# Attention rows cut into two halves, the second half of one row issued beside the first half of the next

## The chip, the cores and the metric

One core of a Trainium2 chip runs the whole program. The metric is the device time of one execution in microseconds (us); lower is better. The engines are TensorE (PE in the profile), VectorE (DVE), ScalarE (ACT), GpSimd (POOL) and SyncE (SP), which here issues most of the DMAs.

## The reference

The input x is float32 of shape 32 x 64 x 112 x 112. Four residual layers follow each other, each on a group-normalised copy of its input:

```
x = x + local_conv(gn(x))          # sign(x) with ternary 3x3 weights
x = x + fourier_mix(gn(x))         # rfft2, complex 64x64 channel mix, irfft2
x = x + conv7x7(gn(x)) + bias      # written as FFTs in the reference
x = x + window_attention(gn(x))    # 8x8 windows, 8 heads of 8 channels
```

The last layer, per window of 64 tokens, is linear attention:

```
q, k, v = split(xw @ qkv_w.T + qkv_b);  k = k + pos_enc
q, k    = relu(q) + eps, relu(k) + eps, both / softplus(scale)
q, k    = cubed, rescaled to their old norms
kv      = k.T @ v (per head);  out = (q @ kv) / (q . mean(k) + eps)
out     = out + depthwise5x5(v);  out = out @ proj_w.T + proj_b
```

## The kernel before

The program has three stages. The first two (local convolution with the forward transform, and the channel mix) end at about 3,230 us of the trace and are not touched. The third, `large_conv_and_attention`, runs over the 32 images and does the inverse transform, the 7x7 convolution and the attention.

An image in this stage has two parts. `bring(n)` makes layer 2's result for image n: 16 groups of first transform products (line 937) that ScalarE copies out (L1077), 14 groups of second products (L950) that VectorE adds to x (L1248), the statistics, and the first four padded chunks of the convolution's input. `both(n)` then runs seven rows. A row does one seventh of image n's convolution on TensorE (204 matmuls of 128x224 in float16, L913) and, between them, one row of 14 windows of attention of image n-1. Matmuls of the convolution are the filler: a table of numbers (`PIECES`, `FIRST_PIECES`, `SECOND_PIECES`) says how many of the 204 have been issued before each attention step.

There is no scheduler. Each engine has its own program, written in order by hand and executed in that order; they meet at counting semaphores. What stands first on an engine holds up everything behind it.

The attention steps of a row l, in the order of TensorE before the change:

- `project` (L976): q, k, v of the 14 windows in four groups into PSUM banks 2 to 5. VectorE's `take_qkv` adds the biases (L1318, L1322) and then does the relu (L1330).
- depthwise product (L992) into banks 4 and 5.
- ScalarE squares q and k (L1152). GpSimd makes the cubes of q (L1480), VectorE those of k (L1346). TensorE transposes the query cubes (L1000); ScalarE copies them to `qt` (L1166).
- ScalarE squares the cubes (L1160), VectorE sums them (L1350), makes the ratio of the norms and scales the keys (L1358).
- key-value products (L1011), masked by VectorE into `kvm` (L1368); numerator (L1023).
- VectorE: reciprocal of the denominator (L1374, L1379), multiply (L1384), add the depthwise result (L1391).
- TensorE transposes the result back (L1031), ScalarE copies it (L1171), TensorE projects it (L1041), ScalarE writes `o2` (L1178, which the profile shows as the tile c_kvm since they share memory), GpSimd adds it to x (L1485), SyncE stores it.

The convolution has its own traffic in a row. It makes nine products p = 0 to 8 in four rotating PSUM banks. ScalarE takes the first three into `bs` (`take_b`, L1141 and L1144). VectorE takes the other six (`take_t`, L1299 and L1302); p = 7 and 8 of a row are taken at the start of the next one. GpSimd's `add_conv` (L1464, L1468) adds them to x, and its second half needs all six takes of that row; when it is done it counts up `x3_done`. `take_b` of the next row waits for that count, since it overwrites `bs`. For the next image's convolution ScalarE pads (L1107), GpSimd and VectorE take differences (L1450 to L1455, L1276, L1277), ScalarE rounds to float16 (`high_part`, L1118), and VectorE keeps the remainder (`low_part`, L1284); the two slots of `tn` are used in turn, so padding chunk k waits for `low_part` of chunk k-2.

## Time and profile before

| | |
|---|---|
| median of 3 runs | 13081.69 us (13077.68 to 13088.68) |
| the profiled execution's own time | 13098.74 us, span of its trace 13097.1 us |
| busy share of the span | PE 81%, PE weight loads 71%, DVE 62%, ACT 45%, POOL 27% |
| convolution matmuls, L913 | 45,696 of them, 5004.8 us busy |
| mean granted TensorE clock | 0.908 |

In a trace row, the first number is the start in us from the span's start, the second the time until the group's last instruction ends, then the engine, the line of the kernel, the operation, out <- in, the shapes and xN, the number of instructions merged. A float32 matmul is recorded as two. In square brackets stands the idle time of that engine just before, and what ended it. Instructions of one engine overlap at their ends by about 0.1 us.

A row of the view of stretches gives the stretch, its length, then the busy time of PE, PE's weight loads, DVE, ACT and POOL, each with its number of instructions, and last the granted TensorE clock (1.00 is 2.4 GHz, 0.50 is 1.2 GHz), the DMA share and GB/s.

### The profile page before, as it was taken

The page shows a single profiled execution, that of the slowest core. Times are in us where ns is not written, and L with a number is a line of the kernel's source. Part 1 is how long each engine was busy: PE and PEld are TensorE (multiplying, and loading weights), DVE is VectorE, ACT ScalarE, POOL GpSimd, SP SyncE. Part 2 cuts the span into 40 slices and gives each one's busy share as a digit, 9 for nine tenths or more (in the row PEclk, how much of TensorE's full clock was granted, in tenths as well). Part 3 has the DMA queues.
Part 4 walks back from the last instruction along what each step waited for, and adds up shares of the span by engine and source line. Part 5 has one row for each costly group of instructions (what it writes and reads, how often), then busy time and mean ns, then how long its engine had stood idle before and what let it go on. Part 6 is the DMA issues. An engine that isn't in the chain of part 4 may idle for free.

```text
span 13097.1 us, 288527 instructions
## 1 busy us (share of the span) xinstructions
PE 10575.0 (81%) x120871; PEld 9276.6 (71%) x120871; DVE 8077.5 (62%) x14156; ACT 5870.0 (45%) x6792; POOL 3544.7 (27%) x2888
## 2 busy tenths in 40 slices
PE   6888878857888888888888888888888888888885
PEld 4666668856777777777777777777777777777774
DVE  6666622144666666666666666666666666666665
ACT  4555521103444445444444444445454444444442
POOL 0000000002333333333333333333333333333331
PEclk9999988878999999999999999999999999999996
DMA  7888889952111111111111111111111111111100
GB/s 187 214 213 220 209 189 240 245 142 54 34 32 33 33 32 34 32 34 32 34 32 33 34 33 44 40 35 32 33 34 32 32 34 32 34 32 34 32 21 15
DMA packets 969161, 946.98 MB, mean 72 GB/s; under 512 B 588704, under 2 KB 933776, under 8 KB 948176
## 3 DMA queue, kind: packets, MB, share of 16 engines
q1 hardware_dynamic: 944400, 708.58, 24.6%
q0 software_dynamic: 23488, 220.21, 4.7%
q8 instruction: 947, 15.52, 0.5%
q14 instruction: 326, 2.67, 0.1%
HBM read 605.77 MB, written 322.96 MB: 71 GB/s over the span
## 4 chain that ended last, share of the span: by engine, by line
PE 31%; DVE 17%; ACT 13%; issue 10%; POOL 4%; DMA 1%; ACTq 0%; DVEq 0%; POOLq 0%; SPq 0%
PE c_ps L913 18%; ACT c_tn L1107 3%; PE c_ps L976 3%; ACT c_xn L1128 2%; PE c_ps L1011 2%; ACT c_kvm L1178 2%; POOL c_cube L1480 2%; PE c_ps L1023 2%; DVE c_s L1350 2%; PE c_ps L1031 2%; DVE c_qk L1330 2%; PE c_ps L1041 2%; DVE c_xp L1284 2%; DVE c_xr L1248 2%; DVE c_inv L1379 1%
## 5 line engine op out<-in xcount | busy, mean ns | idle before, releaser
L913 PE MATMUL c_ps<-c_xp,c_wst 128*128 128x224 f16 x45696 | 5004.8, 268 | 474.4 <-DVE c_xp L1284 474.4
L913 PEld LDWEIGHTS c_ps<-c_xp,c_wst 128*128 128x128 f16 x45696 | 4443.5, 100 | 940.0 <-issue 626.9
L1464 POOL TENSOR_TENSOR c_xr<-c_sm,c_xr 128x448 f32<-128x448 f32 x448 | 616.8, 1377 | 4040.9 <-DVE c_xr L1302 4040.9
L1107 ACT ACTIVATE c_tn<-c_xr,c_nrm 64x448 f32<-64x448 f32 (+1 forms) x960 | 1098.9, 1145 | 145.5 <-DVE c_xp L1284 128.6
L1171 ACT ACTIVATE c_qt<-c_ps 128x896 f32<-128x896 f32 x224 | 205.5, 917 | 2018.1 <-PE c_ps L1031 2018.1
L1450 POOL TENSOR_TENSOR c_tn<-c_tn 128x224 f32<-128x224 f32 (+1 forms) x480 | 594.5, 1239 | 1656.8 <-ACT c_tn L1107 1656.8
L528 PE MATMUL b_ps<-b_xs,b_wt 64*64 64x64 f32 x6384 | 802.5, 299 | 181.1 <-DVE b_xj L504 172.3
L1302 DVE SCALAR_TENSOR_TENSOR c_xr<-c_ps,c_unscale,c_xr 128x224 f32<-128x224 f32 x896 | 546.9, 629 | 611.4 <-PE c_ps L913 611.4
L528 PEld LDWEIGHTS b_ps<-b_xs,b_wt 64*64 64x64 f32 x6384 | 757.5, 219 | 185.5 <-issue 185.3
L1118 ACT ACTIVATE c_xp<-c_tn 128x1080 f16<-128x1080 f32 (+1 forms) x544 | 572.3, 1063 | 662.4 <-DVE c_tn L1277 656.1
L976 PE MATMUL c_ps<-c_wqkv,c_xn 64*128 64x192 f32 x6272 | 757.9, 374 | 118.5 <-ACT c_kvm L1178 62.6
L528 PE MATMUL b_ps<-b_xj,b_wt 64*64 64x64 f32 x6384 | 806.5, 298 | 12.2 <-issue 12.0
L528 PEld LDWEIGHTS b_ps<-b_xj,b_wt 64*64 64x64 f32 x6384 | 767.0, 222 | 13.8 <-issue 13.7
L976 PEld LDWEIGHTS c_ps<-c_wqkv,c_xn 64*128 64x128 f32 x6272 | 547.4, 204 | 289.7 <-issue 92.2
L1178 ACT ACTIVATE c_kvm<-c_ps,c_pbias 64x448 f32<-64x448 f32 x896 | 563.4, 629 | 362.3 <-PE c_ps L1041 353.8
L1480 POOL TENSOR_TENSOR c_cube<-c_sq,c_qk 128x896 f32<-128x896 f32 x224 | 657.7, 2936 | 230.7 <-ACT c_sq L1152 230.7
L1299 DVE SCALAR_TENSOR_TENSOR c_sm<-c_ps,c_unscale,c_bs 128x224 f32<-128x224 f32 x448 | 201.8, 451 | 821.3 <-PE c_ps L913 752.6
L1284 DVE TENSOR_TENSOR c_xp<-c_tn,c_xp 128x1080 f16<-128x1080 f32 (+1 forms) x544 | 695.5, 1290 | 14.2 <-ACT c_xp L1118 14.2
L1318 DVE TENSOR_TENSOR c_qk<-c_ps,c_bqk 128x512 f32<-128x512 f32 (+1 forms) x896 | 557.0, 622 | 236.2 <-PE c_ps L976 228.1
L1152 ACT ACTIVATE c_sq<-c_qk 128x1792 f32<-128x1792 f32 x224 | 380.3, 1698 | 702.9 <-DVE c_qk L1330 702.1
L1350 DVE TENSOR_REDUCE c_s<-c_sq 128x28 f32<-128x1792 f32 x224 | 452.5, 2020 | 384.4 <-ACT c_sq L1160 384.4
L1128 ACT ACTIVATE c_xn<-c_xr,c_nrm 64x448 f32<-64x448 f32 x896 | 675.7, 754 | 24.8 <-DVE c_nrm L1233 15.9
(155 smaller groups left out, 18064.6 us busy)
## 6 DMA issues: line engine op xcount, KB each, us to landing
b_wt<-in_L_conv_weight SPq DMA_DIRECT2D x56, 2048.0 KB, 21.8
a_xc<-in_x SPq DMA_DIRECT2D x64, 1568.0 KB, 18.7
x<-a_x1s POOLq DMA_DIRECT2D x32, 3136.0 KB, 23.1
a_xh<-x SPq DMA_DIRECT2D x64, 1568.0 KB
c_xr<-x SPq DMA_DIRECT2D x32, 3136.0 KB, 11.2
out<-c_xr SPq DMA_DIRECT2D x448, 224.0 KB, 3.1
xf<-a_freq POOLq DMA_DIRECT2D x32, 1792.0 KB, 17.5
b_xs<-xf SPq DMA_DIRECT2D x28, 2048.0 KB, 25.2
```

The costliest lines, as they stand in the source:

```text
L528: ins = pe.matmul(ps[rows, 4 * half + g % 4, at:at + 2 * B], wt[rows, odd, :, f, r], src[rows, odd, :, f], start=(f == lo and r == 0), sto ...
L913: ins = pe.matmul(sums(c, p), wst[:, ws, pr, FIRST_TAP[p] + k].rearrange("p q o -> p (q o)"), xp[:, xs, PLANE[kind] + f, row:row + CROWS, ...
L976: ins = pe.matmul(ps[:, banks[g] + r, 3 * C * (q % 2):3 * C * (q % 2) + 3 * C], xn[rows, 2 * q:2 * q + 2].rearrange("p w t -> p (w t)"), w ...
L1107: ins = act.activation(put[to, :, a - lo:b - lo], get[of, :, a - first:b - first], ACT.Identity, scale=nrm[of, 0, 0:1], bias=nrm[of, 0, 1:2])
L1118: ins = act.activation(xp[:, 0, :, at:at + rows].rearrange("p k j w -> p k (j w)"), tn[:, k % 2, 0:9, 0:rows].rearrange("p k j w -> p k (j ...
L1128: ins = act.activation(xn[C * wr:C * wr + C].rearrange("p w (j hp x) -> p hp j w x", hp=2, x=WS)[:, hp], xr[C * hp:C * hp + C, odd, 8 * a ...
L1178: ins = act.activation(o2[C * hp:C * hp + C].rearrange("p (r b j) x -> p b r j x", r=2, b=2)[:, y], ps[C * y:C * y + C, 4:6, 0:N4].rearran ...
L1284: ins = dve.tensor_tensor(xp[:, 1, :, at:at + rows].rearrange("p k j w -> p k (j w)"), tn[:, k % 2, 0:9, 0:rows].rearrange("p k j w -> p k ...
L1350: dve.tensor_reduce(sums(s6), squares(sq), AX.X, ALU.add).then_inc(s.s6_done, 1)
L1450: pool.tensor_tensor(tn[:, k % 2, E_AT:E_AT + 3:2, 0:hi - lo, 1:1 + QW], tn[:, k % 2, X0_AT:SLOTS:X2_AT - X0_AT, 0:hi - lo, 1:1 + QW], at( ...
L1464: pool.tensor_tensor(here, apart(sm[:, half]).unsqueeze(1).to_broadcast([P, 2, CROWS, QW]), here, ALU.add).then_inc(s.added, 1)
L1480: pool.tensor_tensor(cube[:, :, 0].rearrange("p q r c -> p r q c"), sq[:, :, :, 0], qk[:, :, :, 0], ALU.mult).then_inc(s.q3_done, 1)
```

## The change

The second half of a row, from the numerator to the output, is moved. It is now issued during the first half of the next row (or, for the seventh row of an image, during `bring`). The functions are split for that: `numerator`, `turn_back`, `give_back` on TensorE, `turned` and `give` on ScalarE, `divide`, `multiply`, `add_depthwise` on VectorE, `add_out` on GpSimd.

- Banks: the projection now uses banks 2 and 3 for all four groups, each after VectorE has taken the one before. Depthwise product, key-value products, numerator and the turned result use banks 4 and 5. The first and second transform products use the convolution's four banks.
- The depthwise result is copied out of PSUM by ScalarE (a new 128x896 instruction per row, L1227 of the new kernel), and added by VectorE in one instruction from SBUF where there were two from PSUM.
- `take_b` moves ahead on ScalarE, in front of `turned` and of the square. On VectorE the takes of p = 6, 7, 8 of the row before stand behind the relu; p = 7 and 8 stood in front of `take_qkv`, p = 6 in the row before.
- In `bring`, VectorE's four takes of q, k, v are mixed with the differences and low parts.
- x is loaded in seven pieces, each after the rows of output that it overwrites have been stored, where one load waited for the whole image.
- The table of pieces has new numbers.

That VectorE makes the key cubes is so in both kernels.

The table and TensorE's program:

```
-PIECES = (12, 30, 62, 114, 130, 168, 184)
+PIECES = (14, 26, 38, 52, 72, 112, 188)
...
             def bring(n, odd):
+                row = (n - 1) * A7
+                if above_zero(row):
+                    numerator(row - 1)
...
                 for g in range(16):
+                    if above_zero(row):
+                        if g == 4:
+                            turn_back(row - 1)
+                        if g == 8:
+                            give_back(row - 1)
...
+            def attend(l, a, conv):
+                pieces = PIECES if a else FIRST_PIECES
+                if a:
+                    project(l, 0)
+                    numerator(l - 1)
+                    for g in range(1, 4):
+                        conv(pieces[g - 1])
+                        project(l, g)
+                    conv(pieces[3])
+                    turn_back(l - 1)
+                    conv(pieces[4])
+                    give_back(l - 1)
+                conv(pieces[5])
```

On ScalarE:

```
             def attend(l, a, odd, conv, pad, high):
+                pad()
+                conv(True)
+                if a:
+                    turned(l - 1)
+                act.wait_ge(s.u_done, l + 1)
+                if above_zero(l):
+                    act.wait_ge(s.s6_done, l)
+                    act.wait_ge(s.att_done, l)
+                act.activation(sq[:], qk[:], ACT.Square).then_inc(s.u2_done, 1)
+                if a:
+                    give(l - 1)
+                high(0)
+                conv(False)
```

On VectorE:

```
             def attend(l, a, conv, conv_before, pad, stats):
+                if a:
+                    take_qkv(l, 0)
+                    divide(l - 1)
+                    take_qkv(l, 1)
+                    multiply(l - 1)
+                    take_qkv(l, 2)
+                    add_depthwise(l - 1)
+                    take_qkv(l, 3)
+                    relu(l)
+                conv_before(6)
                 conv_before(7)
                 conv_before(8)
-                if a:
-                    take_qkv(l, a)
```

On SyncE:

```
+            def load_next(t, odd, a):
+                p = (odd + a) % 2
+                sp.wait_ge(out_done[p], (A7 * t + ((A7 * odd + a - p) // 2 + 1)) * 32)
+                sp.nop(nofuse=True)
+                load_x1(2 * t + (2 + odd), odd, a)
```

What stands on TensorE around the two last steps of a row. Before (L1031 turns back, L1041 projects, L976 projects q, k, v of the next row):

```order
L913 MATMUL c_ps<-c_xp,c_wst 128x224 x25
L1031 MATMUL c_ps<-c_ident,c_qt 128x128 [waits c_att_done]
L1031 MATMUL c_ps<-c_ident,c_qt 128x128 x6
L913 MATMUL c_ps<-c_xp,c_wst 128x224 x16
L1041 MATMUL c_ps<-c_qt,c_wproj 64x448 [waits c_back_taken]
L1041 MATMUL c_ps<-c_qt,c_wproj 64x448 x3
```

After (L1010 turns back, L1020 projects; L989 is the fourth projection group of the next row, L1041 its query transposes):

```order
L989 MATMUL c_ps<-c_wqkv,c_xn 128x192 [waits c_qk_taken]
L989 MATMUL c_ps<-c_wqkv,c_xn 128x192
L922 MATMUL c_ps<-c_xp,c_wst 128x224 x10
...
L1010 MATMUL c_ps<-c_ident,c_qt 128x128 [waits c_att_done]
...
L922 MATMUL c_ps<-c_xp,c_wst 128x224 x20
L1020 MATMUL c_ps<-c_qt,c_wproj 64x448 [waits c_back_taken]
...
L922 MATMUL c_ps<-c_xp,c_wst 128x224 x24
...
L1041 MATMUL c_ps<-c_ident,c_cube 128x128 [waits c_q3_done]
```

Both steps have moved from the end of their own row to behind the fourth projection group of the next one; 20 convolution matmuls stand between them where there were 16.

On ScalarE, from the padding at a row's start (L1107 before, L1140 after). Before:

```order
L1107 ACTIVATE c_tn<-c_xr,c_nrm 64x4x4x28 [waits c_lo_done]
...
L1152 ACTIVATE c_sq<-c_qk 128x1792 [waits c_s6_done,c_u_done]
L1128 ACTIVATE c_xn<-c_xr,c_nrm 64x4x14x8 [waits c_qkv_done]
...
L1118 ACTIVATE c_xp<-c_tn 128x9x120 [waits c_prod_done]
...
L1141 ACTIVATE c_bs<-c_ps,c_unscale 128x448 [waits c_x3_done,c_prod_done]
L1160 ACTIVATE c_sq<-c_cube 128x1792 [waits c_s2_done,c_k3_done,c_q3_done]
```

After (L1174 is `take_b`, L1182 `turned`, L1206 the square, L1191 `give`, L1214 the square of the cubes):

```order
L1140 ACTIVATE c_tn<-c_xr,c_nrm 64x4x4x28 [waits c_lo_done]
...
L1174 ACTIVATE c_bs<-c_ps,c_unscale 128x448 [waits c_x3_done,c_prod_done]
L1182 ACTIVATE c_qt<-c_ps 128x896 [waits c_turned_back]
L1206 ACTIVATE c_sq<-c_qk 128x1792 [waits c_att_done,c_s6_done,c_u_done]
L1191 ACTIVATE c_kvm<-c_ps,c_pbias 64x2x224 [waits c_xo_done,c_proj_done]
...
L1151 ACTIVATE c_xp<-c_tn 128x9x120 [waits c_prod_done,c_padded]
...
L1214 ACTIVATE c_sq<-c_cube 128x1792 [waits c_s2_done,c_k3_done,c_q3_done]
```

The instruction that waits for `x3_done` now stands ahead of the copy of the turned result and of the square.

On VectorE, up to the difference behind the relu (L1276 before, L1339 after). Before:

```order
L1299 SCALAR_TENSOR_TENSOR c_sm<-c_ps,c_unscale,c_bs 128x224 [waits c_x3_done,c_prod_done]
L1284 TENSOR_TENSOR c_xp<-c_tn,c_xp 128x9x120 [waits c_hi_done]
L1302 SCALAR_TENSOR_TENSOR c_xr<-c_ps,c_unscale,c_xr 128x224 [waits c_prod_done] x2
L1318 TENSOR_TENSOR c_qk<-c_ps,c_bqk 128x2x256 [waits c_qkv_done]
...
L1330 SCALAR_TENSOR_TENSOR c_qk<-c_qk,c_epsc 128x1792 [waits c_qk_taken]
L1276 TENSOR_TENSOR c_tn<-c_tn 128x12x29 [waits c_differed]
```

After (L1379 takes q and k, L1400 and L1405 divide, L1413 multiplies, L1421 adds the depthwise result, L1393 is the relu, L1362 and L1365 take p = 6, 7, 8):

```order
L1379 TENSOR_TENSOR c_qk<-c_ps,c_bqk 128x2x256 [waits c_qkv_done]
...
L1400 SCALAR_TENSOR_TENSOR c_inv<-c_fac,c_ps 128x56 [waits c_num_done]
...
L1405 RECIPROCAL c_inv<-c_inv 128x112 [waits c_den_done]
...
L1413 TENSOR_TENSOR c_qt<-c_ps,c_inv 128x7x64 [waits c_proj_done,c_inv_done]
...
L1421 TENSOR_TENSOR c_qt<-c_sq,c_qt 128x8x14x8 [waits c_dw_taken,c_mul_done]
L1379 TENSOR_TENSOR c_qk<-c_ps,c_bqk 128x2x128 [waits c_qkv_done]
...
L1393 SCALAR_TENSOR_TENSOR c_qk<-c_qk,c_epsc 128x1792 [waits c_qk_taken]
L1362 SCALAR_TENSOR_TENSOR c_sm<-c_ps,c_unscale,c_bs 128x224 [waits c_x3_done,c_prod_done]
L1365 SCALAR_TENSOR_TENSOR c_xr<-c_ps,c_unscale,c_xr 128x224 [waits c_prod_done] x2
```

The takes of the convolution that stood ahead of the four q, k, v takes now stand behind them, behind three steps of the row before and behind the relu.

## Rows read from the trace of the kernel before

**Rows 1.** Stretches of one image: seven rows, then the time between two images.
```profile
6984.33:7233.76 249.43, 217.63 (x2630) 191.44 (x2630) 171.85 (x286) 118.60 (x139) 95.24 (x72) 0.98 0.05 13
7233.76:7292.86 59.10, 36.32 (x417) 34.36 (x417) 33.86 (x72) 31.23 (x39) 12.15 (x15) 0.75 0.51 125
```

**Rows 2.** Timeline of TensorE, one attention row.
```profile
7363.60 1.81 PE L976 MATMUL c_ps<-c_wqkv,c_xn 64*128 64x192 f32 x16
...
7377.55 0.98 PE L1000 MATMUL c_ps<-c_ident,c_cube 128*128 128x128 f32 x7 [2.79 <-POOL c_cube L1480]
7378.37 5.32 PE L913 MATMUL c_ps<-c_xp,c_wst 128*128 128x224 f16 x52
...
7387.58 1.10 PE L1023 MATMUL c_ps<-c_kvm,c_qt 64*64 64x72 f32 x56 [0.40 <-DVE c_kvm L1368]
...
7394.41 0.98 PE L1031 MATMUL c_ps<-c_ident,c_qt 128*128 128x128 f32 x7 [1.84 <-DVE c_qt L1391]
...
7399.88 1.60 PE L976 MATMUL c_ps<-c_wqkv,c_xn 64*128 64x192 f32 x16
```

**Rows 3.** Timeline of VectorE in and just behind the same row.
```profile
7365.16 0.69 DVE L1318 TENSOR_TENSOR c_qk<-c_ps,c_bqk 128x512 f32<-128x512 f32 x1
...
7369.33 2.10 DVE L1330 SCALAR_TENSOR_TENSOR c_qk<-c_qk,c_epsc 128x1792 f32<-128x1792 f32 x1
...
7390.76 0.33 DVE L1374 SCALAR_TENSOR_TENSOR c_inv<-c_fac,c_ps 128x56 f32<-128x56 f32 x2
...
7392.01 1.16 DVE L1384 TENSOR_TENSOR c_qt<-c_ps,c_inv 128x448 f32<-128x448 f32 x2
...
7400.39 1.15 DVE L1302 SCALAR_TENSOR_TENSOR c_xr<-c_ps,c_unscale,c_xr 128x224 f32<-128x224 f32 x2
```

**Rows 4.** Timeline of GpSimd: the two instructions of one `add_conv`.
```profile
7358.98 1.37 POOL L1464 TENSOR_TENSOR c_xr<-c_sm,c_xr 128x448 f32<-128x448 f32 x1 [20.30 <-DVE c_xr L1302]
7360.49 1.36 POOL L1468 TENSOR_TENSOR c_xr<-c_bs,c_xr 128x448 f32<-128x448 f32 x1
```

**Rows 5.** Timeline of ScalarE: `turned`, `give` and `take_b`.
```profile
7359.35 0.92 ACT L1171 ACTIVATE c_qt<-c_ps 128x896 f32<-128x896 f32 x1 [7.93 <-PE c_ps L1031]
7361.89 2.56 ACT L1178 ACTIVATE c_kvm<-c_ps,c_pbias 64x448 f32<-64x448 f32 x4 [1.62 <-PE c_ps L1041]
...
7377.28 0.64 ACT L1141 ACTIVATE c_bs<-c_ps,c_unscale 128x448 f32<-128x448 f32 x1
```

**Rows 6.** Timeline of TensorE behind the same wait in another image.
```profile
6752.62 1.75 PE L1000 MATMUL c_ps<-c_ident,c_cube 128*128 128x128 f32 x7 [2.83 <-POOL c_cube L1480]
6754.17 7.42 PE L913 MATMUL c_ps<-c_xp,c_wst 128*128 128x224 f16 x52
```

**Rows 7.** Stretch of these rows, with its granted clock.
```profile
6752.00:6758.30 6.30, 5.68 (x30) 4.76 (x31) 4.94 (x9) 3.52 (x5) 0.57 (x1) 0.50 0.00 0
```

**Rows 8.** Timelines of TensorE, VectorE and ScalarE between two images.
```profile
7234.47 12.49 PE L937 MATMUL c_ps<-c_inv_h,c_ys 120*64 120x112 f32 x256 [0.71 <-ACT c_kvm L1178]
...
7292.86 10.16 PE L913 MATMUL c_ps<-c_xp,c_wst 128*128 128x224 f16 x77 [14.57 <-DVE c_xp L1284]
...
7252.22 1.16 DVE L1248 TENSOR_TENSOR c_xr<-c_ps,c_xr 128x448 f32<-128x448 f32 x2 [3.08 <-DMA c_xr<-x]
...
7280.57 2.35 ACT L1107 ACTIVATE c_tn<-c_xr,c_nrm 64x448 f32<-64x448 f32 x2 [1.36 <-DVE c_xp L1284]
...
7286.66 2.34 ACT L1107 ACTIVATE c_tn<-c_xr,c_nrm 64x448 f32<-64x448 f32 x2 [2.62 <-DVE c_xp L1284]
```

**Rows 9.** DMA issues: bytes of each and median us until landed.
```profile
out<-c_xr SPq DMA_DIRECT2D x88, 224.0 KB, 3.1
c_xr<-x SPq DMA_DIRECT2D x6, 3136.0 KB, 11.1
```

**Rows 10.** Timeline of TensorE in the last image's attention, two rows.
```profile
12895.67 1.69 PE L1000 MATMUL c_ps<-c_ident,c_cube 128*128 128x128 f32 x7 [3.14 <-POOL c_cube L1480]
12930.23 1.76 PE L1000 MATMUL c_ps<-c_ident,c_cube 128*128 128x128 f32 x7 [3.09 <-POOL c_cube L1480]
```

More of the change, by code:

```diff
@@ L918, in conv_some, with stats @@
                     at[0] += 1
-            def stats(count):
+            def stats(count, which):
                 pe.wait_ge(s.stats_done, count + 1)
@@ new lines, in bring, with project @@
+                    for g in range(1, 4):
+                        project(row, g)
+            def project(l, g):
+                if g == 0:
+                    pe.wait_ge(s.xn_done, l + 1)
+                    if above_zero(l):
+                        pe.wait_ge(s.qt_taken, l)
+                else:
+                    pe.wait_ge(s.qk_taken, 4 * l + g)
+                for q in range(2 * g, min(2 * g + 2, Q7)):
+                    for r in range(2):
+                        rows = slice(C * r, C * r + C)
+                        ins = pe.matmul(ps[:, 2 + r, 3 * C * (q % 2):3 * C * (q % 2) + 3 * C],
+                                        xn[rows, 2 * q:2 * q + 2].rearrange("p w t -> p (w t)"),
+                                        wqkv[rows].rearrange("p k c -> p (k c)"),
+                                        start=(q % 2 == 0), stop=(q % 2 == 1 or q == Q7 - 1), skip_group_check=True)
+                ins.then_inc(s.qkv_done, 1)
@@ L1017, in attend, with numerator @@
+            def numerator(l):
                 pe.wait_ge(s.kvm_done, 2 * l + 2)
@@ L1055, in last @@
             def last(n, odd):
-                if above_zero(n * A7):
-                    pe.wait_ge(s.t_taken, n * (A7 * NT))
-                stats(2 * n - 1)
-                project((n - 1) * A7, 0, range(4))
+                row = (n - 1) * A7
+                numerator(row - 1)
+                turn_back(row - 1)
+                give_back(row - 1)
+                pe.wait_ge(s.qt_taken, row)
+                stats(2 * n - 1, 1)
+                for g in range(4):
+                    project(row, g)
                 for a in range(A7):
-                    attend((n - 1) * A7 + a, a, lambda k: None)
+                    attend(row + a, a, lambda k: None)
+                numerator(row + A7 - 1)
+                turn_back(row + A7 - 1)
+                give_back(row + A7 - 1)
             image_steps(pe, B, bring, both, last)
@@ L1199, in last @@
             def last(n, odd):
+                turned(n * A7 - (A7 + 1))
+                give(n * A7 - (A7 + 1))
                 deviation(2 * n - 1)
@@ L1424, in last @@
                     dve.wait_ge(s.bn3_done, n * CHUNKS)
+                row = (n - 1) * A7
+                divide(row - 1)
+                multiply(row - 1)
+                add_depthwise(row - 1)
                 norm(1, 2 * n - 1, bn3)
-                take_qkv((n - 1) * A7, 0)
+                for g in range(4):
+                    take_qkv(row, g)
+                relu(row)
                 for a in range(A7):
-                    attend((n - 1) * A7 + a, a, lambda p: None, lambda p: None, lambda what, k: None, lambda: None)
+                    attend(row + a, a, lambda p: None, lambda p: None, lambda what, k: None, lambda: None)
+                divide(row + A7 - 1)
+                multiply(row + A7 - 1)
+                add_depthwise(row + A7 - 1)
             image_steps(dve, B, bring, both, last)
```

347 lines of the change are left out of this document (179 added, 168 removed).

## The prediction, made before the changed kernel was run

> **What bounds the kernel now.** I read the page first: TensorE is busy 81% of the span and no other engine comes near. Then the stretches of one image, since the third stage repeats 31 times with attention [rows 1]: seven rows take 249.4 us, of which TensorE is busy 217.6, and the stretch to the next image's first convolution matmul takes 59.1, of which it is busy 36.3. So the two places to look at are TensorE's idle time in a row, and the path between two images, where TensorE is no bound.
>
> The timeline of one row [rows 2] lasts 7399.88 - 7363.60 = 36.28 us and has three idle gaps: 2.79 before the query transposes (GpSimd's cubes), 0.40 before the numerator, 1.84 before the transposes back (VectorE). That is 5.03; TensorE's own work in a row is 36.28 - 5.03 = 31.25. The change aims at these gaps. If all went, six rows of every image would gain 5 us each, 31 x 30 = 930 us.
>
> **A row after the change.** I lay out one row from the start of its first projection group, with durations of [rows 2 to 5], engine by engine.
>
> TensorE issues, up to `give_back`: four projection groups (1.81 for two, so 3.0 for three and a half), numerator 1.1, turn back 0.8, and 72 convolution matmuls at 5.32/52 = 0.102, 7.4 us. It is at `give_back` at 12.3. Behind that stand 31.25 - 12.3 = 18.95 us of work.
>
> VectorE takes the first group at 1.0 to 2.0 (four groups start at 7365.16 and end at 7369.33, with one wait of 0.4 inside, so a full one is about 1.0 and the half one 0.7), divides (7392.01 - 7390.76 = 1.25) to 3.3, takes the second at 4.4 to 5.4, multiplies (1.16) to 6.6, takes the third to 7.6. Adding the depthwise result is now one instruction of 896 from SBUF. The trace has no such instruction; bounds are the two PSUM adds it replaces, as long as the multiply's 1.16, and half of that, and I take 1.1: to 8.7. The fourth take ends at 9.4, the relu (2.1) at 11.5. Only then come p = 6, 7, 8 of the row before: two cost 1.15, so three at most 1.7; I take 1.5, to 13.0.
>
> GpSimd's second `add_conv` needs these takes. It lasts 7360.49 + 1.36 - 7358.98 = 2.87, to 15.9, and I add 0.4 because VectorE's differences run beside it: 16.3 (bounds 15.9 and 17.0). That counts up `x3_done`.
>
> ScalarE's `take_b` waits for `x3_done` and stands ahead of everything else in the row. It ends at 16.9 (0.6), `turned` at 17.8 (0.92). TensorE's `give_back` waits for `turned`: it is there at 12.3 and starts at 17.8. So a wait of 5.5 us takes the place of the three of 5.0. Queued behind it on TensorE are 132 convolution matmuls, the query transposes, the depthwise and the key-value products; behind it on ScalarE the square, and behind that both cubes.
>
> Is anything later still? The square ends at 19.5, GpSimd's cubes at 22.4, and TensorE reaches the query transposes at 17.8 + 0.9 + 4.1 = 22.8: no wait. `give` (2.56) is done at 22.1, before the depthwise products. The second square, the sums, a low part, and the scaling end near 30.5; the depthwise copy, a new ScalarE instruction that I price like `turned` at 0.92 (bounds 0.6 and 1.3), near 30.5 too. The key-value products come at 33.4. The new copy is hidden. The mask is ready before the next row's numerator. So a row lasts 17.8 + 18.95 = 36.75 at full clock, 0.5 more than now.
>
> **The clock.** After the wait of 2.83 us in another image [rows 6] the transposes took 1.75 us where they take 0.98, and the 52 matmuls behind them 7.42 where they take 5.32: 2.9 us lost, the granted clock at 0.50 for six us, that is 1.2 GHz for 2.4 [rows 7]. In [rows 2] a wait of 2.79 cost nothing. So such a wait costs 0 or 2.9 us; after the 14.57 us between images 77 matmuls take 10.16 for 7.9, 2.3 lost [rows 8]. With 5.5 us of idle in every row I expect the clock to fall in nearly all rows, and take 2.0 us a row (bounds 0 and 2.9). The Trainium skill (TensorE: Matmul & The Clock Gate, section HAM oscillation) describes this as a pattern: a wait that comes back in every tile makes every tile start cold. By that rule all rows pay, which agrees with rows 6 and 7; rows 2 show that a shorter wait can be free. A row is then 36.75 + 2.0 = 38.7.
>
> **The first row of an image** loses its second half, and gets the depthwise products (1.8), which stood in the idle stretch ahead. 204 x 0.104 + 0.8 + 1.8 + 1.7 (key-value products) + 2.2 for the low clock at its start = 27.4. Nothing else is late there: 100 matmuls stand ahead of the query transposes. Seven rows: 27.4 + 6 x 38.7 = 259.6, against 249.4 [rows 1]: +10.2 an image, x 31 = **+316**.
>
> **Between two images.** Two terms.
>
> First, the last row's second half is now in `bring`. VectorE reaches `divide` only after p = 8 (0.8 after the last convolution matmul), GpSimd's 2.9, and two statistics of 1.1: at 4.9. Divide, multiply and add end at 8.4. TensorE has done four of the sixteen groups (12.49/16 = 0.78 each [rows 8]) by 4.2 and waits 4.2 us for the transposes back, and again the clock may fall. ScalarE, which copies each group in 0.82, inserts `turned` (0.92) and `give` (2.56). I get `give` done at 17.9. GpSimd adds it (2.1) by 20.1, two stores are issued and land (0.6 each, 3.1 [rows 9]) at 24.4, and the last piece of x may load. A load of 448 KB is not in the trace: bounds are 3.1 (a store of 224 KB) and 11.1 (the whole of x, seven pieces) [rows 9]. I take 3.7, nearer to the store, since the bytes are nearer. VectorE's first x add, which waits for all seven pieces, starts at 28.2 after the last convolution matmul, where it is 7252.22 - 7233.76 = 18.5 now [rows 1, 8]: +9.7, in 30 images **+291**. The load in pieces thus wins nothing: its last piece waits for a row of output that now comes later. The Trainium skill (DMA: Bandwidth & Descriptors, section Anatomy of one DMA) gives about 2.0 us fixed and 436 GB/s; by its estimate the piece takes 3.0 us, and this term would be 0.7 us smaller an image; no row here shows one.
>
> Second, the chain of padded chunks. Now VectorE takes all of q, k, v and the relu before the first difference, and then the chain pad, difference, round, remainder goes round in 7286.66 - 7280.57 = 6.1 us for each of chunks 2 and 3 [rows 8]. After the change difference 0 and low part 0 stand between the takes: low part 0 ends some 2.8 us earlier, low part 1 directly follows its rounding instead of difference 2. I lay it out at 5.8 us earlier for the first convolution matmul (bounds 2.8 and 7): 31 x 5.8 = **-180**.
>
> **The last image** has attention only. Its rows come every 12930.23 - 12895.67 = 34.56 us at low clock [rows 10]. With the second half beside the next row I count 27.5 for a row: 7 x 7 = **-49**, here the change does what it says.
>
> **Sum.** +316 + 291 - 180 - 49 = +378 us. The profiled execution took 13098.74 us (span 13097.1); the median shown is 17 less. 13098.7 + 378 - 17 = 13460.
>
> **Rivals.**
> A. The wait at `give_back` is there, but the clock holds. For it: rows 2. Against: the wait is twice as long. Rows of 36.75: 27.4 + 220.5 = 247.9, -1.5 x 31 = -47; sum -47 + 291 - 180 - 49 = +15: 13097.
> B. The overlap works: the takes, `add_conv`, `take_b` and `turned` are done before TensorE is at `give_back`, and rows come near to TensorE's 31.25, say 32.3 with a residue of one. For it: 5.0 us of idle and VectorE is free in much of the row. Against: the chain above has five links, each with its row, and would have to be 5.5 us shorter. 27.4 + 193.8 = 221.2, -28.2 x 31 = -874; with the other terms -812: 12270. If the chain were only 2 us shorter, a row would be 34.8 and hold its clock: about 12730. A says where this decides: with the clock held, every row shorter than 36.7 is a gain; with the clock lost, only one whose wait is over 2 us shorter.
> C. Contention and a second wait come on top: `add_conv` and the differences slow each other more, the key cubes come late, or the clock falls also in the stretch between images. Rows of 40 (6 x 1.3 x 31 = 242 more) and 3 us more in between (93): 378 + 242 + 93 = +713: 13790.
>
> **How the numbers follow.** My layout 0.60 (13460, its own range 13250 to 13650); A 0.13; B, full or in part, 0.16; C 0.11. Differences of 0.2% (26 us) are about what a measurement of this kernel can tell from none. A lies within it in half of its cases or less, and slightly above zero: same 0.06, faster 0.18, slower 0.76. The range 13080 to 13760 leaves out B and the top of C.
>
> **What would show it.** TensorE should show one gap of about 5.5 us a row ahead of the 64x448 products (L1020), ended by ScalarE's L1182, and hardly any at the query transposes; the granted clock in the rows should be below 0.98. On ScalarE L1174 should wait for GpSimd's L1553, some 4 us or more. Between images, VectorE's L1302 (the x add) should still wait for the DMA. If the row shows gaps at L1010 or L1041 instead, my order of the chain is wrong; if TensorE's largest gap is under 3 us, the forecast is wrong in sign.

## The result: 2.3% slower, and the profile after

The changed kernel takes 13395.82 us (median of 4 runs, 13391.28 to 13399.15) beside 13085.19 us of the kernel before on the same chip: ratio 1.0234, 95% interval 1.0216 to 1.0252. The forecast was 13460. The profiled execution took 13399.15 us (span 13397.5, before 13097.1), at a mean granted clock of 0.889 where it was 0.908.

TensorE's timeline of one attention row, the answer to [rows 2] (start, length, engine, line, operation, count, and in brackets the idle time ahead and what ended it):

```profile
7227.32 0.92 PE L989 MATMUL c_ps<-c_wqkv,c_xn 64*128 64x192 f32 x8
7228.17 1.11 PE L1002 MATMUL c_ps<-c_kvm,c_qt 64*64 64x72 f32 x56
...
7236.94 0.93 PE L1010 MATMUL c_ps<-c_ident,c_qt 128*128 128x128 f32 x7
7237.70 2.14 PE L922 MATMUL c_ps<-c_xp,c_wst 128*128 128x224 f16 x20
7245.52 1.77 PE L1020 MATMUL c_ps<-c_qt,c_wproj 64*64 64x448 f32 x8 [5.67 <-ACT c_qt L1182]
7247.22 6.15 PE L922 MATMUL c_ps<-c_xp,c_wst 128*128 128x224 f16 x40
7253.21 0.93 PE L1041 MATMUL c_ps<-c_ident,c_cube 128*128 128x128 f32 x7
```

The three gaps of before are gone. In their place is one of 5.67 us ahead of `give_back` (L1020), in every row but the first of an image. Behind it the eight products take 1.77 us for 0.98, and 40 convolution matmuls 6.15 for 4.14: the low clock. `give_back` of six rows starts at 7169.34, 7207.42, 7245.52, 7284.71, 7322.94 and 7360.44: 38.2 us a row in this image. Over all 31 images that have both parts, the wait is 4.8 to 5.7 us (mean 5.25) in each of the 186 rows, the products behind it run at the low clock every time, and a row takes 37.96 us in the mean. The granted clock in the seven rows of an image is 0.93 in the mean, where it was 0.97.

The three engines that the gap goes back to, in one timeline (the answer to [rows 3 to 5]):

```profile
7236.55 2.02 DVE L1393 SCALAR_TENSOR_TENSOR c_qk<-c_qk,c_epsc 128x1792 f32<-128x1792 f32 x1
7238.49 0.44 DVE L1362 SCALAR_TENSOR_TENSOR c_sm<-c_ps,c_unscale,c_bs 128x224 f32<-128x224 f32 x1
7238.85 1.12 DVE L1365 SCALAR_TENSOR_TENSOR c_xr<-c_ps,c_unscale,c_xr 128x224 f32<-128x224 f32 x2
7240.12 1.92 POOL L1549 TENSOR_TENSOR c_xr<-c_sm,c_xr 128x448 f32<-128x448 f32 x1 [10.63 <-DVE c_xr L1365]
7242.19 1.35 POOL L1553 TENSOR_TENSOR c_xr<-c_bs,c_xr 128x448 f32<-128x448 f32 x1
7243.93 0.63 ACT L1174 ACTIVATE c_bs<-c_ps,c_unscale 128x448 f32<-128x448 f32 x1 [15.98 <-POOL c_xr L1553]
7244.47 0.91 ACT L1182 ACTIVATE c_qt<-c_ps 128x896 f32<-128x896 f32 x1
```

Read it from above: relu, the three takes, the two additions of `add_conv`, `take_b`, `turned`. Each starts where the one above ends. ScalarE stood still for 15.98 us ahead of `take_b`, although the transposes back, which `turned` copies, had been done since 7237.9.

Over the whole program, two groups of the page:

```profile
L1174 ACT ACTIVATE c_bs<-c_ps,c_unscale 128x448 f32<-128x448 f32 x224 | 141.7, 633 | 3164.3 <-POOL c_xr L1553 3131.7
L1020 PE MATMUL c_ps<-c_qt,c_wproj 64*64 64x448 f32 x1792 | 369.6, 910 | 985.0 <-ACT c_qt L1182 985.0
```

Between two images (the last convolution matmul ends at 7380.5), TensorE and VectorE, the answer to [rows 8]:

```profile
7381.49 3.29 PE L954 MATMUL c_ps<-c_inv_h,c_ys 120*64 120x112 f32 x64
7389.06 1.76 PE L1010 MATMUL c_ps<-c_ident,c_qt 128*128 128x128 f32 x7 [4.27 <-DVE c_qt L1421]
...
7446.74 3.44 PE L922 MATMUL c_ps<-c_xp,c_wst 128*128 128x224 f16 x20 [10.52 <-DVE c_xp L1347]
...
7384.32 1.15 DVE L1372 BATCH_NORM_STATS2 c_bn<-c_xr 128x6 f32<-128x448 f32 x2 [3.10 <-POOL c_xr L1553]
...
7410.65 1.16 DVE L1302 TENSOR_TENSOR c_xr<-c_ps,c_xr 128x448 f32<-128x448 f32 x2 [3.95 <-DMA c_xr<-x]
```

and the load of a piece in the DMA issues (count, bytes, median us to landing), the answer to [rows 9]:

```profile
c_xr<-x SPq DMA_DIRECT2D x224, 448.0 KB, 4.1
```

**Where the 300 us of the spans come from.** The first convolution matmul beside attention, and that of the last image that has both, in the kernel before:

```profile
3247.69 10.35 PE L913 MATMUL c_ps<-c_xp,c_wst 128*128 128x224 f16 x77 [14.69 <-DVE c_xp L1284]
...
12584.07 9.92 PE L913 MATMUL c_ps<-c_xp,c_wst 128*128 128x224 f16 x77 [14.49 <-DVE c_xp L1284]
```

and after:

```profile
3252.62 7.62 PE L922 MATMUL c_ps<-c_xp,c_wst 128*128 128x224 f16 x50 [10.44 <-DVE c_xp L1347]
...
12917.75 11.64 PE L922 MATMUL c_ps<-c_xp,c_wst 128*128 128x224 f16 x100 [10.44 <-DVE c_xp L1347]
```

Thirty periods: 311.2 us each before, 322.2 after, +329. The start is 5 us later, the last seven rows with convolution are 3.5 longer, and the last image's attention ends 37 us sooner. Together +300. Of the +11.0 in a period, +7.3 lie between the images and +3.6 in the seven rows: over all images of the two traces, the stretch between images takes 66.9 us in the mean for 59.6, and the seven rows 255.3 for 251.6. The image of [rows 1], with 249.4 us, was the shortest of the 31 of the kernel before; the longest took 255.9. The 5 us of the start are no effect of the change that can be told, since this first matmul comes anywhere from 3225.8 to 3269.6 us in the traces of this document.

### The profile page after: what moved, and what is told of

Its sections match the earlier page's. It is cut to its first block, busy times and chain, and to the rows that moved or that the text cites. A ratio compares the mean times of both kernels' runs of the same rounds, so it can differ in the third digit from the quotient of the medians.

```text
span 13397.5 us, 290073 instructions
## 1 busy us (share of the span) xinstructions
PE 10745.4 (80%) x120871; PEld 9299.3 (69%) x120871; DVE 7950.3 (59%) x13932; ACT 6026.8 (45%) x7016; POOL 3465.6 (26%) x2888
## 4 chain that ended last, share of the span: by engine, by line
PE 43%; DVE 13%; issue 8%; POOL 6%; ACT 4%; DMA 2%; DVEq 0%; SPq 0%; POOLq 0%; ACTq 0%
PE c_ps L922 27%; PE c_ps L989 3%; PE c_ps L1062 3%; PE c_ps L1049 3%; POOL c_xr L1549 3%; PE c_ps L1020 2%; POOL c_xr L1553 2%; DVE c_v L1383 2%; DVE c_qt L1413 2%; DVE c_qt L1421 2%; DVE c_xr L1365 2%; PE c_ps L1002 2%; DVE c_xr L1302 1%; PE c_ps L1041 1%; ACT c_qt L1182 1%
## 5 line engine op out<-in xcount | busy, mean ns | idle before, releaser
L1549 POOL TENSOR_TENSOR c_xr<-c_sm,c_xr 128x448 f32<-128x448 f32 x448 | 756.0, 1687 | 4041.2 <-DVE c_xr L1365 4041.2
L1174 ACT ACTIVATE c_bs<-c_ps,c_unscale 128x448 f32<-128x448 f32 x224 | 141.7, 633 | 3164.3 <-POOL c_xr L1553 3131.7
L1020 PE MATMUL c_ps<-c_qt,c_wproj 64*64 64x448 f32 x1792 | 369.6, 910 | 985.0 <-ACT c_qt L1182 985.0
L1140 ACT ACTIVATE c_tn<-c_xr,c_nrm 64x448 f32<-64x448 f32 (+1 forms) x960 | 1098.5, 1144 | 116.7 <-DVE c_xp L1347 101.8
L989 PE MATMUL c_ps<-c_wqkv,c_xn 64*128 64x192 f32 x6272 | 821.2, 378 | 172.6 <-DVE c_v L1383 165.1
L1444 DVE TENSOR_TENSOR c_cube<-c_sq,c_qk 128x896 f32<-128x896 f32 x224 | 244.7, 1093 | 1179.9 <-ACT c_sq L1206 1179.9
L1379 DVE TENSOR_TENSOR c_qk<-c_ps,c_bqk 128x512 f32<-128x512 f32 (+1 forms) x896 | 558.0, 623 | 599.5 <-PE c_ps L989 599.0
L528 PE MATMUL b_ps<-b_xj,b_wt 64*64 64x64 f32 x6384 | 801.4, 298 | 19.9 <-issue 19.8
L1020 PEld LDWEIGHTS c_ps<-c_qt,c_wproj 64*64 64x64 f32 x1792 | 69.4, 186 | 1033.8 <-issue 1029.5
L989 PEld LDWEIGHTS c_ps<-c_wqkv,c_xn 64*128 64x128 f32 x6272 | 533.9, 201 | 361.6 <-DVE c_v L1383 278.3
L1535 POOL TENSOR_TENSOR c_tn<-c_tn 128x224 f32<-128x224 f32 (+1 forms) x480 | 341.3, 711 | 1651.0 <-ACT c_tn L1140 1645.9
L1553 POOL TENSOR_TENSOR c_xr<-c_bs,c_xr 128x448 f32<-128x448 f32 x448 | 739.2, 1650 | 64.2
L278 DVE SCALAR_TENSOR_TENSOR a_x1s<-a_ps,a_alph,a_xc 64x448 f32<-64x448 f32 x896 | 612.4, 683 | 129.4 <-PE a_ps L374 110.4
```

Source lines behind the costliest of these rows:

```text
L278: ins = dve.scalar_tensor_tensor(x1s[rows, ROWS * c:ROWS * c + ROWS], ps[rows, c % 3, 0:N4].rearrange("p (a w) -> p a w", a=ROWS), alph[ro ...
L528: ins = pe.matmul(ps[rows, 4 * half + g % 4, at:at + 2 * B], wt[rows, odd, :, f, r], src[rows, odd, :, f], start=(f == lo and r == 0), sto ...
L989: ins = pe.matmul(ps[:, 2 + r, 3 * C * (q % 2):3 * C * (q % 2) + 3 * C], xn[rows, 2 * q:2 * q + 2].rearrange("p w t -> p (w t)"), wqkv[row ...
L1020: ins = pe.matmul(ps[C * y:C * y + C, 4 + r, 0:N4], wproj[rows], att_t[rows].rearrange("p w (y x) -> p y w x", y=WS)[:, 4 * y:4 * y + 4], ...
L1140: ins = act.activation(put[to, :, a - lo:b - lo], get[of, :, a - first:b - first], ACT.Identity, scale=nrm[of, 0, 0:1], bias=nrm[of, 0, 1:2])
L1549: pool.tensor_tensor(here, apart(sm[:, half]).unsqueeze(1).to_broadcast([P, 2, CROWS, QW]), here, ALU.add).then_inc(s.added, 1)
```

## Experiments

The runs stand on different chips, each beside runs of the kernel before on its own chip, so differences are taken between ratios to the kernel before, times 13085 us. Each interval is about 0.0015 wide to either side, 20 us. Where a mean over all images is given, it is taken from the whole trace.

**takes_first.** In VectorE's `attend`:

```
+                conv_before(6); conv_before(7); conv_before(8)
                 if a:
                     take_qkv(l, 0)
...
                     relu(l)
-                conv_before(6); conv_before(7); conv_before(8)
```

> VectorE takes p = 6, 7, 8 of the row before ahead of the first take of q, k, v instead of behind the relu; nothing else changes. My theory (the chain relu, takes, GpSimd's second add_conv, ScalarE's take_b, turned sets give_back): x3_done comes about 5 us after the row's start instead of 16.5, the wait of 5.4 to 5.7 us ahead of L1020 falls below 0.5, the granted clock in the rows goes to 0.98 or more, and a row is then bound by TensorE's own 31.25 us plus a wait of 0.4 for the query cube (relu 1.3 us later): 32.2 for 38.1. 5.9 x 6 rows x 30 images = -1060 us: about 12340 (12200 to 12550). Rival 1, VectorE is too full for a row of 32 (it is busy 29.5 us of a row): the gap moves to the query transposes or the key-value products, row 34 to 36: 12640 to 13000. Rival 2, the cost is the sharing of the two banks or the clock and not this chain: the wait at L1020 stays over 4 us and the time stays above 13200.

Measured: 12058.23 us, ratio 0.9209 (0.9194 to 0.9224): 1340 us less than the changed kernel, and below the expected range. TensorE's timeline:

```profile
7227.02 0.98 PE L1020 MATMUL c_ps<-c_qt,c_wproj 64*64 64x448 f32 x8
7231.91 0.93 PE L1041 MATMUL c_ps<-c_ident,c_cube 128*128 128x128 f32 x7
7232.68 1.94 PE L1049 MATMUL c_ps<-c_v,c_spread 128*128 128x112 f32 x16
7242.09 1.78 PE L1062 MATMUL c_ps<-c_v,c_cube 64*64 64x72 f32 x56
7246.31 1.10 PE L1002 MATMUL c_ps<-c_kvm,c_qt 64*64 64x72 f32 x56
7257.92 0.98 PE L1020 MATMUL c_ps<-c_qt,c_wproj 64*64 64x448 f32 x8
```

No line has a bracket: a row is 30.9 us (7257.92 - 7227.02), all of it TensorE's work, as the stretch of one row shows (length, busy time of TensorE, its weight loads, VectorE, ScalarE, GpSimd, and then the granted clock):

```profile
7242.00:7272.90 30.90, 30.90 (x384) 27.46 (x382) 25.43 (x44) 19.60 (x23) 14.79 (x12) 1.00 0.12 32
```

The order of three VectorE instructions was the whole of the loss in the rows, and more. The stretch between images stays as long as in the changed kernel (66.3 us in the mean for 66.9). Both rivals fall: VectorE has 5.5 us to spare even here. I had expected 32.2, with a wait of 0.4 at the query transposes that does not come and with 31.25 for TensorE's own work, which is 30.9.

**take_b_later.** In ScalarE's `attend`:

```
                 pad()
-                conv(True)
                 if a:
                     turned(l - 1)
...
                 high(0)
+                conv(True)
                 conv(False)
```

> ScalarE's take_b of the first two products, which waits for x3_done, is moved from ahead of turned and the square to behind give and the first high part; VectorE's order is as in the changed kernel. My theory: turned then waits only for the transposes back, and the wait ahead of L1020 goes (under 0.5 us). But GpSimd's query cube still stands behind its second add_conv, which still waits for the takes behind the relu: that ends 16.3 us after the row's start, the cube (2.97) at 19.3, where TensorE is at the query transposes at 17.3: a wait of about 2.0 us there. Row 33.3 for 38.1: -4.8 x 180 = -870, about 12530 (12350 to 12750); so 150 to 250 us slower than takes_first. Rival, take_b itself is then late for the sums (GpSimd, VectorE's t of p = 3): the gain is lost again at the 76 matmuls' waits, above 12900. Rival 2, as in takes_first: no change.

Measured: 12488.93 us, ratio 0.9539 (0.9523 to 0.9555), as expected; 430 us slower than takes_first where 150 to 250 were expected, since takes_first came out better.

```profile
7224.17 0.98 PE L1020 MATMUL c_ps<-c_qt,c_wproj 64*64 64x448 f32 x8
7230.94 0.98 PE L1041 MATMUL c_ps<-c_ident,c_cube 128*128 128x128 f32 x7 [1.72 <-POOL c_cube L1571]
...
7257.00 0.98 PE L1020 MATMUL c_ps<-c_qt,c_wproj 64*64 64x448 f32 x8
```

The chain can be cut at this link too. `give_back` waits no more, but GpSimd's cube, still behind `add_conv`, is late by 1.72 us: a row of 32.8 us here, and of 33.7 in the mean, since in 37 of 217 rows the query transposes ran at the low clock behind such a wait.

**give_back_later.** `PIECES = (14, 26, 38, 52, 112, 112, 188)` for `(14, 26, 38, 52, 72, 112, 188)`.

> Only the place of give_back on TensorE changes: 60 instead of 20 convolution matmuls stand between the transposes back and give_back, and none between give_back and the query transposes. My theory, a chain of fixed length sets the row, not give_back's place: give_back is reached at 16.6 instead of 12.5 us and waits 1.5, and the query transposes then wait for the square and the cube, 3.5 to 4 us (ended by GpSimd L1571). Row 37.5 to 38.5: time within 1% of the changed kernel, perhaps 100 to 200 us less where two short waits keep the clock up. Rival, give_back's place is the fault: the wait goes, rows of 33 to 34, about 12600.

Measured: 13354.33 us, ratio 1.0202 (1.0185 to 1.0219), 40 less than the changed kernel.

```profile
7224.27 0.98 PE L1020 MATMUL c_ps<-c_qt,c_wproj 64*64 64x448 f32 x8 [1.74 <-ACT c_qt L1182]
7228.92 1.76 PE L1041 MATMUL c_ps<-c_ident,c_cube 128*128 128x128 f32 x7 [3.67 <-POOL c_cube L1571]
```

The gap splits in two that add to 5.4 again, and the low clock comes behind the second. The place of `give_back` is not the fault.

**clock_kept.** TensorE works where it waited:

```
                     conv(pieces[4])
+                    pe.wait_ge(s.qk_taken, 4 * l + 4)
+                    for _ in range(50):
+                        pe.matmul(ps[:, 2, 0:NQ], <128x128 of wst>, <128x224 of wst>, start=True, stop=True, ...)
                     give_back(l - 1)
```

> Ahead of give_back in the second to seventh row of an image TensorE issues 50 matmuls more (128x224 f16 from the weights, into a bank that is free there), some 5.1 us, so that it works where it waits in the changed kernel; their results are not used. My theory: the wait of 5.4 to 5.7 us costs itself and then a low clock (1.77 us instead of 0.9 for the L1020 products, 6.15 instead of 4.1 for the 40 matmuls behind them): give_back starts at the same time, the rest of a row is 1.0 to 1.4 us shorter, 180 to 250 us less in all (13150 to 13220), though 9000 matmuls are added. Rival, the clock falls for another reason than the wait: no change or slower, and L1020 still takes 1.77.

Measured: 13057.76 us (9 runs), ratio 0.9975 (0.9965 to 0.9986): 339 us less than the changed kernel and more than expected, and even 0.25% faster than the kernel before. The matmuls added are 9600 and not 9000: 50 in six rows of all 32 images.

```profile
7120.93 4.95 PE L1038 MATMUL c_ps<-c_wst 128*128 128x224 f16 x50
7126.17 0.98 PE L1020 MATMUL c_ps<-c_qt,c_wproj 64*64 64x448 f32 x8 [0.28 <-ACT c_qt L1187]
7127.08 4.14 PE L922 MATMUL c_ps<-c_xp,c_wst 128*128 128x224 f16 x40
7131.06 0.93 PE L1046 MATMUL c_ps<-c_ident,c_cube 128*128 128x128 f32 x7
```

`give_back` starts at 7090.13, 7126.17, 7162.55 and 7198.36, 36.1 us apart. Over all images a row takes 36.3 us for 37.96, and the stretch from `give_back` to the query transposes 4.9 for 6.6: the low clock costs 1.7 us a row. The rows thus give 311 of the 341 us between the two spans. The stretches between images give 37, and the start 14, which is within what it varies by; the 300 matmuls in the last image, beside which there is no convolution, cost 20. I expected 1.0 to 1.4 us a row because I had read one row only, from `give_back` at 7207.42 to the next projection at 7227.32: 19.9 us. In the next row, whose 1.77 and 6.15 us the expectation quotes, the same stretch takes 21.2 (7245.52 to 7266.76), and in clock_kept 18.4.

**turn_first.** At the end of an image:

```
                 take_t(n, odd, A7 - 1, 8)
+                divide(...); multiply(...); add_depthwise(...)   # of the last row, out of bring and last
                 x3_stats(n, odd, A7 - 1)
```

> The changed kernel with one move at the end of an image: VectorE divides, multiplies and adds the depthwise result of the last row right behind the takes p = 6, 7, 8, ahead of the last statistics of x3, which wait for GpSimd. My theory: the wait of 4.27 us ahead of the transposes back between images falls to about 0.5, the 64 matmuls behind it take 3.3 instead of 5.3, give ends 4 to 5 us earlier and with it the stores and the last load: the first x add starts at about 25.7 us after the last convolution matmul instead of 30.2. -4.5 x 30 = -135: about 13260 (13200 to 13310). Rival, the x add hangs on something else (the statistics of x3 come 3.5 us later on VectorE, their chain then ends last): no change within 30 us.

Measured: 13222.41 us, ratio 1.0114 (1.0099 to 1.0130), 157 less than the changed kernel. The wait is 0.53 us and the x add comes 23.1 us behind the transform's first matmul (29.2 in the changed kernel):

```profile
7287.82 3.29 PE L954 MATMUL c_ps<-c_inv_h,c_ys 120*64 120x112 f32 x64
7291.64 0.98 PE L1010 MATMUL c_ps<-c_ident,c_qt 128*128 128x128 f32 x7 [0.53 <-DVE c_qt L1418]
...
7310.90 1.16 DVE L1299 TENSOR_TENSOR c_xr<-c_ps,c_xr 128x448 f32<-128x448 f32 x2 [4.37 <-DMA c_xr<-x]
```

6.1 us gained there, where 4.5 were expected: ScalarE's copies of the transform behind `turned` also came earlier, and with them `give`. Over all 30 stretches between images the gain is 5.2 us in the mean (25.5 us behind the last convolution matmul for 30.8), which makes the 157. It is smaller in 13 of them, for a reason that all_three shows below.

**last_piece.** A semaphore of its own for the seventh piece of x:

```
-                dve.wait_ge(x1_in[odd], 8 * A7 * (n + (2 - odd)))
+                dve.wait_ge(x1_in[odd], 8 * (A7 - 1) * (n + (2 - odd)))
                 for c in range(CHUNKS):
+                    if c == CHUNKS - 2:
+                        dve.wait_ge(x1_late[odd], 8 * (n + (2 - odd)))
```

> The changed kernel, but the seventh piece of x counts up a semaphore of its own, and VectorE waits for it only ahead of the thirteenth of the fourteen x adds. My theory: the first x add no longer waits for the DMA (3.95 us in the trace) but starts when the first products of the second transform are there, about 7407.0 instead of 7410.65 in the stretch read: -3.7 x 30 = -110: about 13285 (13250 to 13320), and no wait ahead of the thirteenth. Rival, VectorE's adds are limited by TensorE behind them, and half of this or less arrives: above 13340.

Measured: 13301.10 us, ratio 1.0166 (1.0151 to 1.0182), 89 less. The x add still waits for a DMA:

```profile
7359.31 1.16 DVE L1305 TENSOR_TENSOR c_xr<-c_ps,c_xr 128x448 f32<-128x448 f32 x2 [1.68 <-DMA c_xr<-x]
```

So the theory holds in part: the seventh piece did hold up the add, but not it alone. What is left is the sixth piece, which SyncE loads behind the seventh row's stores; sixth_piece below shows it. The gain is 20 us smaller than expected.

**cubes_back.** takes_first with `k3_done` counted by GpSimd, whose second product `cube[:, :, 1]` stands behind the first.

> The order of takes_first with the key cubes made by GpSimd again, behind the query cube, as in the kernel before. In takes_first the key-value products start 3.3 us behind the scaled keys, and GpSimd's query cube ends 1.1 us before its transposes. My theory: the keys' cube ends 3 us later, the scaling 1.6 us later, which is still before the key-value products: no change within 30 us of takes_first (12030 to 12090), the move to VectorE is worth nothing by itself. Rival, it is what makes room on GpSimd: GpSimd's output add and add_conv come 3 us later and show at take_b or at the output stores: 100 us or more slower than takes_first.

Measured: 12071.37 us, ratio 0.9233 (0.9219 to 0.9247), 0.0024 above takes_first and on another chip. The two intervals just overlap, and the profiled executions have spans of 12061.9 and 12061.4 us. So no difference that these runs can tell. The expectation is wrong in one point: in the kernel before, too, VectorE makes the key cubes, so this run undoes nothing of the change.

**all_three.** takes_first, turn_first and last_piece together.

> takes_first, turn_first and last_piece in one kernel. If the two terms between images add, the first x add starts at about 21 us after the last convolution matmul for 30 to 31: -9 x 30 = -270 from takes_first: about 11790 (11730 to 11870). Rival, the two overlap (both shorten the same wait for the last piece): only -135, about 11920.

Measured: 11846.24 us (5 runs), ratio 0.9053 (0.9040 to 0.9065): 204 less than takes_first, between the two numbers.

```profile
7273.36 3.29 PE L955 MATMUL c_ps<-c_inv_h,c_ys 120*64 120x112 f32 x64
...
7291.59 8.57 PE L967 MATMUL c_ps<-c_inv_w,c_xp 128*128 128x112 f32 x60 [1.75 <-ACT c_xp L1111]
...
7293.55 0.62 DVE L1302 TENSOR_TENSOR c_xr<-c_ps,c_xr 128x448 f32<-128x448 f32 x1 [1.48 <-DMA c_xr<-x]
7295.05 0.62 DVE L1302 TENSOR_TENSOR c_xr<-c_ps,c_xr 128x448 f32<-128x448 f32 x1 [0.88 <-PE c_ps L967]
```

The x add comes 20.2 us behind the transform's first matmul for 29.2, as expected, but then the adds wait for TensorE one by one (0.88): 37.1 us from the first add to the convolution for 36.1 (36.8 in the mean over all images). That gives back about 20 us of the 270. Some 50 more are lost in 13 of the 30 stretches between images, where TensorE starts the numerator 2.1 to 3.9 us late, with no wait for another engine that the profile shows ("issue"):

```profile
7000.71 1.11 PE L1003 MATMUL c_ps<-c_kvm,c_qt 64*64 64x72 f32 x56 [2.35 <-issue]
```

They are the 13 places where the kernel's loop over pairs of images goes back to its start, and no others. What holds TensorE there no run shows. The x add comes 25.2 us behind the last convolution matmul in these and 21.3 in the other 17; 3.8 x 13 = 50. In takes_first the same delay costs nothing (30.2 us in both kinds), because the wait ahead of the transposes back hides it.

**whole_x.** The 448 KB loads replaced by one of 3136 KB behind the last store.

> The changed kernel with x loaded whole again (3136 KB in one DMA, when all seven rows of output are stored), as in the kernel before; everything else stays. My theory: the load starts at the same time as the seventh piece does now but lands 11.1 us behind its issue instead of 4.1, so the first x add starts at 37 instead of 30.2 us after the last convolution matmul: +7.0 x 30 = +210: about 13605 (13560 to 13650). So the pieces win 7 us an image, and it is the place of the last row's second half alone that loses 12. Rival: the whole load is hidden or its landing time is shorter on the free queues: no change within 50 us.

Measured: 13577.26 us, ratio 1.0370 (1.0354 to 1.0386), 178 more than the changed kernel. The x add comes 37.2 us behind the last convolution matmul in the mean, for 30.8, so the pieces win some 6 us an image.

```profile
7153.14 1.15 DVE L1295 TENSOR_TENSOR c_xr<-c_ps,c_xr 128x448 f32<-128x448 f32 x2 [11.44 <-DMA c_xr<-x]
```

**takes_then_differ.** In VectorE's `bring`: all `take_qkv`, `relu`, and then the rounds of `differ` and `low_part` as in the kernel before.

> The changed kernel, but between images VectorE takes all of q, k and v and does the relu before the first difference of the padded chunks, and rounds go difference k+1, low part k, as in the kernel before. My theory: the time from the first x add to the first convolution matmul, 36.1 us in the changed kernel and 40.6 before, goes back to 40.6 or a little more: +4.5 to +5.8 x 31 = +140 to +180: about 13550. Rival: the takes and the order of the differences change nothing, it is another part of the change that shortened this stretch: within 40 us of the changed kernel.

Measured: 13633.40 us, ratio 1.0414 (1.0398 to 1.0430), 236 more: beyond both theories. The first x add is at 7179.29, the convolution at 7223.29: 44.0 us, not 40.6.

```profile
7197.02 0.69 DVE L1373 TENSOR_TENSOR c_qk<-c_ps,c_bqk 128x512 f32<-128x512 f32 x1
...
7199.86 0.69 DVE L1373 TENSOR_TENSOR c_qk<-c_ps,c_bqk 128x512 f32<-128x512 f32 x1 [1.75 <-PE c_ps L989]
```

Two takes start 2.84 us apart. In the kernel before the first two were 1.0 apart (7269.96 and 7270.96) and the fourth began 3.8 us behind the first, since its projections had two pairs of banks and ran ahead; here it begins 7.9 us behind. With the one pair of the change each group waits for the take of the one before. So this part of the change has two halves: the mixed order wins 7.9 us (44.0 - 36.1), which this run shows, and 3.4 (44.0 - 40.6) are lost again, which these rows put down to the single pair of banks; no run has the changed kernel with two pairs. 4.5 are left.

**sixth_piece and relu_behind.** SyncE's `load_next(t, odd, a - 1)` ahead of `wait_ge(s.xo_done, ...)`; and on top of it `relu(row)` behind `differ(n, 2)`.

> all_three, and SyncE issues the load of piece a - 1 ahead of its wait for row a's output instead of behind row a's stores; so the sixth piece no longer stands behind the seventh row's output. In all_three the first x add still waited 1.3 to 1.5 us for a DMA. My theory: that wait goes, -1.3 x 30 = -40 at most, and about half of it is given back since TensorE's second transform paces the adds there (they wait 0.9 us for it one by one): 11820 (11800 to 11850). Rival: no change.

> sixth_piece, and between images VectorE's relu of the first row moves from ahead of low part 1 to behind the difference of chunk 2. In the trace of all_three GpSimd's differences beside this relu take 1.48 and 1.43 us where they take 0.67 and 0.39 alone, and the chain to the first convolution matmul goes through them. My theory: the first convolution matmul comes 0.6 to 1.8 us earlier, 20 to 55 us less than sixth_piece: about 11785. Rival: the chain goes through ScalarE's copies, and the slower GpSimd beside the relu is hidden: within 15 us.

Measured: 11847.33 us, ratio 0.9045 (0.9032 to 0.9057), and 11835.94 us, 0.9038 (0.9025 to 0.9050). Neither can be told from all_three. In sixth_piece the wait for the DMA is gone, and the adds wait for TensorE's second transform (`L967`) from the first on. In relu_behind the third difference takes 0.67 us where it took 1.47, but from the first add to the convolution it is 36.6 us for 37.0 in the mean: GpSimd's slower differences beside the relu are nearly all hidden, as the rival had it. About 11840 us, 9.5% below the kernel before, is the best version found.

## Why the forecast was right, and which of its terms were not

**The new wait: right.** Forecast 5.5 us ahead of `give_back`, ended by `turned`, `give_back` 17.8 us behind the row's first projection; measured 4.8 to 5.7, and 18.2. takes_first and take_b_later each cut one link of the chain and the wait went; give_back_later left the chain whole and moved the wait. So the cause is shown.

**The clock: right, its price a little too high.** 2.0 us a row forecast, 1.7 by clock_kept. Rival A, the wait without the clock, was thus run: 36.3 us a row, 13058 us; the forecast gave it 36.75 and 13097. The Trainium skill (TensorE: Matmul & The Clock Gate, section HAM oscillation) says that every tile pays for a wait that comes back in each; by that rule all rows pay, and the trace agrees: the clock fell in all 186 rows, though the price per row was 1.7 us in the mean and not the 2.9 of [rows 6].

**The rows' term: much too large,** +316 forecast, +113 measured (255.3 us for 251.6, in 31 images). The forecast had 259.6 for 249.4, and both numbers are off. A row is 37.96 us and not 38.7, which is 4.4 us in six rows: 0.3 us a row from the clock, and the rest from the row itself, at most 36.3 at full clock for 36.75. The first row, 27.0 in one image (12917.75 to 12944.75) and 27.5 by the means, is as forecast, although the terms that the forecast lists for it add up to 27.7 and not to 27.4. The other 2.2 us are the baseline: [rows 1] is the fastest image of the kernel before, at a clock of 0.98, and the others already lost clock in their gaps.

**The x add: too small,** +9.7 forecast, +11.9 measured (30.8 us behind the last convolution matmul in the mean for 18.9), 357 us for 291. The turn back waits 4.27 us as forecast (4.2), but in the stretch shown `give` is done at 19.2 instead of 17.9, and the piece takes 4.1 us and not 3.7. The estimate of 3.0 by the Trainium skill (DMA: Bandwidth & Descriptors, section Anatomy of one DMA) is further off; the section gives its figures for DMAs that GpSimd issues, and these are issued by SyncE. The forecast also said that the pieces win nothing: whole_x shows that they win 6 us an image. They do not make up for the later output of the last row.

**The chain of padded chunks:** -5.8 forecast, -4.6 measured (-137 for -180 us). The sum left out the single pair of banks (3.4 us) and priced the mixed order at 5.8 where it wins 7.9.

**The last image:** -37 for -49. Between five of its rows it is 26.0 us in the mean (L1010 from 13230.13 to 13360.33), shorter than the 27.5 forecast, but ahead of them stands the last row's second half with waits of 7.46 us for VectorE and 7.47 for ScalarE.

Measured, the terms are +113 + 357 - 137 - 37 and +5 for the start: +301. The errors are -203 in the rows and +126 in the rest. So the wait, its place and the sign were forecast rightly, but that 13460 lies only 64 us above the measured 13396 is in part luck, two errors that cancel.

**Rival B** gave 12270 for an overlap that works. takes_first, in which it does, takes 12058.

## What to carry to other kernels

When work is interleaved by hand, follow the in-order queues of all engines: the three gaps that this change removed came back as one, because ScalarE had an instruction ahead of the copy TensorE needed that waited for the other task's GpSimd, which waited for VectorE. Put each engine's last duties of the old round ahead of those of the new one, or behind nothing that a third engine waits for. And take a baseline from the mean of many periods, not from the one that is read.
